# A threshold search in a two-layer kernel: counting on VectorE, or comparing on VectorE and adding up on TensorE

## The reference

```python
# layer 0, attention: 8 heads of 16
scores = einsum('bhqd,bhkd->bhqk', q, k) * scale * 1.25
threshold = top_k(scores, 102)[0][..., -1:]        # the 102nd largest of each row of 512
scores = scores * where(scores >= threshold, 1.24, 1.0)
li = conv1d(scores.mean(axis=-2), conv_w) + conv_b
probs = softmax(scores * li[:, :, None, :]);  x = x + ga * (probs @ v @ Wo + bo)
# layer 0, experts: all 8 experts on all tokens, mixed with top-2 weights
# layer 1: a Mamba block (a scan over 512 tokens, 256 channels, 16 states),
#          then 8 experts that each see at most 153 tokens of a batch (gather, three products, scatter)
```

## Time and profile before

| | us |
|---|---|
| median of three runs | 3173.97 (3163.5 to 3178.97) |
| the profiled execution, its own time | 3173.85 |
| its span in the trace | 3172.5 |
| VectorE busy | 2473.1 (78%) |
| TensorE busy | 2230.1 (70%) |
| ScalarE busy | 1472.9 (46%) |
| GpSimd busy | 1231.8 (39%) |

### The profile page before, as it was taken

The page is one execution under the profiler, slowest core; times in us unless marked ns, Lnnn a source line. Parts: engine busy times, 40 slices in busy tenths (PEclk is TensorE's granted clock), DMA queues, the critical chain, the costliest instruction groups (busy, mean ns, idle before and its releaser), DMA issues. The chain is left out here.

```text
span 3172.5 us, 33555 instructions
## 1 busy us (share of the span) xinstructions
PE 2230.1 (70%) x8648; PEld 1159.3 (37%) x8767; DVE 2473.1 (78%) x6145; ACT 1472.9 (46%) x3124; POOL 1231.8 (39%) x1118
## 2 busy tenths in 40 slices
PE   4168775877767777687768778677868778758644
PEld 2025221553235522454225532345325432435213
DVE  5874888869887799978889797889889897853472
ACT  3317613665245733567236732567236743724322
POOL 1020345414453054523545144532535144534461
PEclk7579786998878788897979889788969889869757
DMA  4011113141132212332121312323122321313223
GB/s 98 1 29 28 29 32 93 44 112 59 52 86 59 90 51 62 95 80 71 51 82 63 97 52 62 92 66 97 51 75 68 95 62 46 97 49 105 77 64 92
DMA packets 137460, 215.11 MB, mean 68 GB/s; under 512 B 17873, under 2 KB 57441, under 8 KB 134113
## 3 DMA queue, kind: packets, MB, share of 16 engines
q1 hardware_dynamic: 133088, 203.88, 22.6%
q0 software_dynamic: 4096, 8.40, 1.0%
HBM read 190.06 MB, written 22.15 MB: 67 GB/s over the span
## 5 line engine op out<-in xcount | busy, mean ns | idle before, releaser
L1370 POOL TENSOR_TENSOR gat<-sil,cbs 128x512 f32<-128x512 f32 x256 | 324.6, 1271 | 214.1 <-PE ps_rest L1300 109.6
L1335 ACT ACTIVATE sil<-ps_rest,w_b1T 128x512 f32<-128x512 f32 x256 | 175.5, 687 | 426.9 <-PE ps_rest L1310 405.0
L768 DVE TENSOR_SCALAR_CACHE_REDUCE wmask<-z,tc 128x512 bf16<-128x512 f16 x512 | 349.8, 740 | 30.3 <-ACT z L735 28.3
L1021 PE MATMUL ps_att<-z,Vp 128*32 128x128 f32 x2048 | 280.2, 283 | 46.0 <-DVE z L1093 33.5
L937 POOL TENSOR_SCALAR wmask<-wmask 128x512 bf16<-128x512 bf16 x256 | 164.3, 642 | 375.2 <-DVE wmask L894 369.3
L1310 PE MATMUL ps_rest<-rest_hT,WF 128*128 128x512 f32 x512 | 289.1, 652 | 16.1 <-ACT sil L1335 16.1
L1300 PE MATMUL ps_rest<-gat,WP 128*128 128x512 f32 x512 | 276.9, 625 | 12.2 <-POOL gat L1370 11.6
L1622 POOL TENSOR_TENSOR rest_c<-rest_c,hg 128x512 f32<-128x512 f32 x128 | 162.3, 1268 | 315.4 <-DVE hg L1581 315.4
L1549 ACT ACTIVATE ps_rest<-cols,Aneg 128x512 f32<-128x512 f32 x256 | 175.5, 688 | 225.4 <-DVE hfc L1569 197.6
L1021 PEld LDWEIGHTS ps_att<-z,Vp 128*32 128x32 f32 x2048 | 208.4, 112 | 135.3 <-issue 113.4
L1526 PE MATMUL ps_rest<-hg,ident 128*128 128x512 f32 x256 | 183.8, 808 | 102.9 <-DVE hg L1581 102.6
(11 more groups left out here) (347 smaller groups left out, 4976.5 us busy)
## 6 DMA issues: line engine op xcount, KB each, us to landing
cbs<-spreads SPq DMA_DIRECT2D x128, 256.0 KB, 3.6
ccs<-spreads SPq DMA_DIRECT2D x128, 256.0 KB, 3.3
WF<-in_w SPq DMA_DIRECT2D x64, 256.0 KB, 2.7
WP<-in_w SPq DMA_DIRECT2D x64, 256.0 KB, 2.7
WF<-in_wfc SPq DMA_DIRECT2D x64, 256.0 KB, 2.7
WG<-in_wgate SPq DMA_DIRECT2D x64, 256.0 KB, 3.0
WP<-in_wproj SPq DMA_DIRECT2D x64, 256.0 KB, 3.1
qk<-bounce SPq DMA_DIRECT2D x32, 384.0 KB, 5.8
```

The source lines that it names most:

```text
L768: od.up(dve.tensor_scalar(wmask[:, i, :], z_at[i], tc[:, 0, i:i + 1], None, ALU.is_ge, ALU.add, accum_out=tc[:, 1, i:i + 1]))
L1021: mm = pe.matmul(obank[o:o + 32, a * P:(a + 1) * P], Vp[:, kc, h, :], pT[u][:, kc, :], start=kc == 0, stop=kc == NT - 1)
L1370: weighed0.up(pool.tensor_tensor(gat[m % 2], sil[m % 2], cbs[e % 2][:], ALU.mult))
```

## The change

A tile is counted on VectorE no more in one instruction. VectorE writes the mask alone (`tensor_scalar` with `is_ge` and no `accum_out`). TensorE then takes the masks of a group of tiles, `FOLDS`, through an identity matrix: for a group of 16 tiles it multiplies, 16 times over, a slice of 32 columns of each mask, and accumulates all in one PSUM bank, so that 512 columns hold 32 partial sums for each tile. Groups of 8 or 6 tiles take slices of 64 columns, 8 times over. VectorE reduces each bank to counts with one `tensor_reduce`. Groups by round: 16 and 8 tiles, 16 and 6, 16 and 6, then 16, 8 and 8. ScalarE counts 8, 10, 10 and 0 tiles, in place of 8, 14, 14 and 0. The new generator `pe_search` stands in TensorE's list and waits there for the last compare of a group (`cut`), in round 0 also for the end of the refill before the second group; `dve_search` waits for the products (`spread`). `weave` is given 459.0 and a lead of 1.25 for the attention chain. Two more GpSimd instructions at the start make the identity in bf16.

```diff
-SIGNS = (8, 14, 14, 0)
+SIGNS = (8, 10, 10, 0)
 SLOPE = 1.0 / 140.0
 ROUNDS = len(SIGNS)
+FOLDS = {22: ((0, 16), (16, 22)), 24: ((0, 16), (16, 24)), 32: ((0, 16), (16, 24), (24, 32))}
+FOLD_W = {16: 32, 12: 32, 10: 32, 8: 64, 6: 64}
...
+    ident_bf = sb("ident_bf", [P, P], BF16)
...
+    cut, spread = sig("cut", sum(TILES - n for n in SIGNS)), sig("spread", sum(len(FOLDS[TILES - n]) for n in SIGNS))
...
+        built.up(pool.memset(ident_bf[:], 0.0)); pool.wait_ge(*built.at(0, 18))
+        built.up(pool.affine_select(out=ident_bf[:], in_=ident_bf[:], compare_op=ALU.not_equal, fill=1.0, base=0,
+                                    pattern=[[-1, P]], channel_multiplier=1))
...
+    def fold_bank(n):
+        return att.bank[3 - n]
+
+    def cut_before(k):
+        return sum(TILES - n for n in SIGNS[:k])
+
+    def spread_before(k):
+        return sum(len(FOLDS[TILES - n]) for n in SIGNS[:k])
+
+    def pe_search(b):
+
+        for k in range(ROUNDS):
+            for n, (lo, hi) in enumerate(FOLDS[TILES - SIGNS[k]]):
+                if k == 0 and n == 0 and b:
+                    yield attended.at(b - 1)
+                    pe.wait_ge(*attended.at(b - 1))
+                if k == 0 and n == 1:
+                    yield zed.all(b)
+                    pe.wait_ge(*zed.all(b))
+                yield cut.at(b, cut_before(k) + hi - 1)
+                pe.wait_ge(*cut.at(b, cut_before(k) + hi - 1))
+                w = FOLD_W[hi - lo]
+                to = fold_bank(n)[:, 0:(hi - lo) * w].rearrange("p (i w) -> p i w", w=w)
+                for c in range(S // w):
+                    mm = pe.matmul(to, ident_bf[:], wmask[:, lo:hi, c * w:(c + 1) * w], start=c == 0, stop=c == S // w - 1)
+                    if c == S // w - 1:
+                        spread.up(mm)
+                    yield 0.26
...
                     dve.wait_ge(*zed.at(b, i))
-                od.up(dve.tensor_scalar(wmask[:, i, :], z_at[i], tc[:, 0, i:i + 1], None, ALU.is_ge, ALU.add,
-                                        accum_out=tc[:, 1, i:i + 1]))
-                yield 0.67
+                cut.up(dve.tensor_scalar(wmask[:, i, :], z_at[i], tc[:, 0, i:i + 1], None, ALU.is_ge))
+                yield 0.27
+            for n, (lo, hi) in enumerate(FOLDS[TILES - SIGNS[k]]):
+                w = FOLD_W[hi - lo]
+                yield spread.at(b, spread_before(k) + n)
+                dve.wait_ge(*spread.at(b, spread_before(k) + n))
+                od.up(dve.tensor_reduce(tc[:, 1, lo:hi], fold_bank(n)[:, 0:(hi - lo) * w].rearrange("p (i w) -> p i w", w=w), AX.X, ALU.add))
+                yield 0.66
...
+    def pe_searches():
+        for b in every:
+            yield from pe_search(b)
...
-           (453.0, 1.1, (("pe", pe_choices()), ("act", act_choices()), ("dve", dve_choices()), ("pool", pool_choices()),
+           (459.0, 1.25, (("pe", pe_choices()), ("act", act_choices()), ("dve", dve_choices()), ("pool", pool_choices()),
                          ("pe", pe_attention()), ("act", act_attention()), ("dve", dve_attention()), ("pool", pool_attention()),
-                         ("sp", sp_attention()), ("pe", pe_prepares()), ("act", act_prepares()), ("dve", dve_prepares()), ("pe", pe_refills()), ("act", act_refills())))),
+                         ("sp", sp_attention()), ("pe", pe_prepares()), ("act", act_prepares()), ("dve", dve_prepares()), ("pe", pe_refills()), ("act", act_refills()), ("pe", pe_searches())))),
```

More of the change, by code:

```diff
@@ L136, in emit @@
     loaded, late = sig("loaded", len(EARLY) + 1, 16), sig("late", len(LATER), 16, 30.0)
-    built, hot, cleared = sig("built", 18), sig("hot", 8), sig("cleared", 8 * FULL + 2 * E + 7)
+    built, hot, cleared = sig("built", 20), sig("hot", 8), sig("cleared", 8 * FULL + 2 * E + 7)
     siluc, modp, bop, ready = sig("siluc", 2), sig("modp", 2), sig("bop"), sig("ready", 5)
```

## The result

The changed kernel takes **3417.14 us** (median of 4 runs, 3416.52 to 3429.65) against 3174.52: a ratio of 1.078 (95% interval 1.074 to 1.082), slower by 243 us. The forecast was 3095, with a range of 3010 to 3200 and a chance of 0.18 for slower.

The account below looks back on a forecast made before the run. VectorE was the fullest engine (2473 of 3172 us), though none was full over the whole span. Terms of -14 - 4 - 1.4 + 5 + 3 = -11.4 us a batch, -80 for seven, gave 3095 us, range 3010 to 3200.

Parts of the forecast that it names:

- Order and lead: Attention chain's lead of 1.25 for 1.1: attention at most 54 us earlier, costed at 0, with 20 us either way.
- The rest of the sum: All terms but the lead: -14 - 4 - 1.4 + 5 + 3 = -11.4 us a batch, -80 for seven.
- Counts, compares, reductions, ScalarE: Search: VectorE -61.4 + 27.0 + 5.9 = -28.5 us a batch; eight ScalarE counts fewer, -5.6, counted as -1.4.
- TensorE: 104 added products a batch in the search, taken at 0.275 us each, mostly in idle time: 3 us a batch show.
- Round latency: Search rounds 1 to 3 end behind the products yet get shorter: -14 us a batch, between -8.3 and -20.3.
- The second rival: No change: rounds wait for products in TensorE's list, so the gains sum to zero, 3174 us; chance 0.17.
- Collision with GpSimd: Beside exp0, GpSimd keeps 250 compares waiting 0.25 us each, 62 us in all; counted as +5 us a batch.
- The third rival: Slower: GpSimd keeps VectorE's compares out in rounds 2 and 3 beside exp0, 3254 or 3304 us; chance 0.18.

Follow-up runs that it names:

- constant lead: Changed kernel with attention's planned work per batch set to 435.6 in place of 459.0, so 1.25 does not grow over the batches: 3093.24 us, ratio 0.976.
- the Identity pair: Changed kernel with exp0's Silu replaced by Identity: 3319.38 us with 459.0 and 1.25, 3096.59 us with 435.6 and 1.25.
- the cut of TensorE's work: Changed kernel, exp0's second product for 128 of 512 columns: 3233.48 us at 459.0, 1.25 with Identity for Silu; 3067.97 us at 453.0, 1.1 with Silu.
- the same repair: Kernel before with attention's planned work 443.1 and 1.25 in place of 453.0 and 1.1: 3088.72 us, ratio 0.976.
- the old settings: Changed kernel with 453.0 and a lead of 1.1, as in the kernel before, in place of 459.0 and 1.25: 3143.81 us, ratio 0.992.
- the run at 3247: Changed kernel with compares that still sum, into an unused tile, with 475.6 planned and a lead of 1.25 that does not grow: 3247.40 us, ratio 1.024.

## Why the prediction was wrong

**The step that failed** is "Order and lead", costed at 0 with 20 us either way. It cost 273 us: 3417 against 3144, the changed kernel with the new settings and with the old ones. Against a constant lead it is 324. I took the lead for a shift of at most 54 us, a question of how long the end is. I did not add up the planned work, so I missed that 459.0 makes the lead grow, to 1.66 at the last batch where the kernel before has 1.28, and I did not ask which stages would meet. The end that I had named but priced at nothing went from 376 to 484 us. Two more of the things that follow could be read ahead of time: that Silu and Exp alternate on one engine, from the lines of ScalarE's list, and that the scan needs VectorE for 69 of 73 us and exp0 TensorE for 60 of 62, so that each must lie beside something that leaves this engine free.

Of the 324 us the loads are 98, shown by the Identity pair. The 223 of the distance are shown as a sum, and that 112 of them lie in the end is read from the traces. That the others come from stages that want the same engine side by side is what the stretches suggest; the cut of TensorE's work didn't prove it, and what does most there stays open.

**The rest of the sum** came out at 3093 against the 3095 of the forecast (its terms add up to 3094), and that is luck: the kernel before comes to 3089 by the same repair, and at the old settings the change was worth 30 us (3144), not 80. So the other terms failed in size too. The two pages at the constant lead, kernel before and changed kernel:

```profile
PE 2200.5 (71%) x8767; PEld 1136.5 (37%) x8767; DVE 2449.8 (79%) x6145; ACT 1473.9 (48%) x3124; POOL 1229.5 (40%) x1118
```

```profile
PE 2365.4 (76%) x9599; PEld 1210.5 (39%) x9599; DVE 2258.7 (73%) x5545; ACT 1431.5 (46%) x2996; POOL 1235.8 (40%) x1120
```

VectorE has 191 us less to do and the span is 11 us longer (3082.7 and 3094.0; the medians differ by 4).

- *Counts, compares, reductions, ScalarE:* right in size. 0.27 a compare, 0.684 a reduction, VectorE's busy sum down by 183 where 165 was forecast.
- *TensorE:* a product takes 0.22 as said, and the busy sum rose by 152 to 165, less than the 180 to 350 forecast. By themselves the products cost 25 us; I had 3 us a batch, 21 in seven. In the first batch's rounds the granted clock is 0.75, where it was 0.50 with TensorE idle:

```profile
83.00:136.00 53.00, 24.59 (x87) 9.69 (x88) 35.13 (x133) 15.99 (x46) 0.47 (x1) 0.75 0.00 1
```

- *Round latency:* wrong. I had rounds 1 to 3 shorter by 14 us, 9 with the collision. At a constant lead the three rounds of batch 4 go from 1372.80 to 1456.89 in the kernel before and from 1362.49 to 1443.46 in the changed one, 84.1 and 81.0 us. Batches 2 to 7 are alike, about 3 us a batch less in the mean. Round 1 even grew, from 26.9 to 37.7. In the changed kernel itself batch 3 took 18.6, 21.4 and 27.7 us, where 16 to 18 twice and 18 were forecast, but ahead of exp0, which starts at 1130.7 there, and not beside it. The timeline of VectorE in the changed kernel, constant lead, from the end of round 0 to that of round 1:

```profile
1362.49 0.17 DVE L816 TENSOR_SCALAR tc<-tc 128x8 f32<-128x8 f32 x1
...
1378.93 0.34 DVE L804 TENSOR_SCALAR wmask<-both_parts,tc 128x512 bf16<-128x512 f16 x1
...
1397.87 0.69 DVE L810 TENSOR_REDUCE tc<-ps_att 128x16 f32<-128x512 f32 x1 [0.89 <-PE ps_att L785]
...
1400.22 0.16 DVE L816 TENSOR_SCALAR tc<-tc 128x10 f32<-128x10 f32 x1
```

and TensorE's in the same kernel:

```profile
1373.35 0.59 PE L785 MATMUL ps_att<-wmask,ident_bf 128*128 128x512 bf16 x2
...
1374.94 0.38 PE L785 MATMUL ps_att<-wmask,ident_bf 128*128 128x512 bf16 x1
1375.19 0.53 PE L1793 MATMUL ps_rest<-cols,WF 128*128 128x153 f32 x2
...
1392.36 0.38 PE L785 MATMUL ps_att<-wmask,ident_bf 128*128 128x512 bf16 x1
...
1393.52 1.89 PE L785 MATMUL ps_att<-wmask,ident_bf 128*128 128x512 bf16 x8
...
1397.46 0.86 PE L785 MATMUL ps_att<-wmask,ident_bf 128*128 128x512 bf16 x4
...
1362.00:1400.00 38.00, 33.87 (x196) 28.17 (x197) 27.18 (x94) 23.93 (x61) 2.05 (x2) 0.88 0.40 123
```

  The last compare ends at 1379.3; the reduction starts 18.6 us later. The 24 products want 5 us, but they stand in pieces among the products of exp1 (L1793): three run by 1375.3, the next only at 1392.36, with 17 us of exp1 between, on a TensorE that is busy for 34 of 38 us (last row, busy by stretch). I had priced the products back to back, at 0.275 each. The second rival had this mechanism, rounds that wait for TensorE; its price, no change, is what the constant lead shows.
- *Collision with GpSimd:* right in kind, and the size, 70 us of VectorE's time against 62, fits by luck. I had 250 compares beside exp0 at 0.25 more each. In the changed kernel none lies in exp0. There 71 take over 0.6 us, about 1 us more each, all beside GpSimd's products of the scan (L1650, L1663):

```profile
1775.30 1.26 POOL L1663 TENSOR_TENSOR rest_c<-rest_c,hg 128x512 f32<-128x512 f32 x1 [7.93 <-DVE hg L1622]
1776.50 2.72 DVE L804 TENSOR_SCALAR wmask<-z,tc 128x512 bf16<-128x512 f16 x2
1776.52 1.27 POOL L1650 TENSOR_TENSOR rest_c<-cols,cbs 128x512 f32<-128x512 f32 x1
1777.74 1.32 POOL L1650 TENSOR_TENSOR gat<-cols,cbs 128x512 f32<-128x512 f32 x1
```

  At the constant lead rounds do lie beside exp0, and the excess is 21 us over all compares (mean 372 ns), a third of the forecast, with 9 compares over 0.6 us. The third rival, slower by this collision, is refuted as the main cause: the kernel before, whose counts were never hit, loses 147 us by the same settings. But the 49 us between 70 and 21 are VectorE time in a scan where VectorE is nearly full, so a part of the 223 us may be theirs. No run separates it.

## What to carry to other kernels

When independent chains share the engines, decide which stages may lie side by side before anything is tuned: by the engine each fills, and by the function table ScalarE needs in each. A number that sets the order (a lead, a total of planned work) must be made anew with every change of a planned duration, and a change has to be compared with the kernel before at the best order found for each; else it is the order that is measured, up to 324 us here against 30 at the old settings and 4 at the constant lead for the change. Work that is moved to another engine's queue costs the wait behind what stands there, not its own duration.

## What the runs showed of the hardware

- Two ScalarE functions from two tables cost 1.283 us at each change, and next to nothing beside it: in the timeline above a load starts 0.02 us behind the accumulator's read (2404.07 + 0.19 to 2404.28), and the activation follows 1.29 us after it. The Trainium skill (ScalarE: Activation LUTs, § What ACT_TABLE_LOAD costs) gives the same 1283 ns and a drain of about 1380 more; that drain is not seen here, and the measurement decides. In time the 180 loads were worth 98 us.
- An instruction of the fast form waits for GpSimd where the summing form of the same comparison never did: up to 1.445 us against a median of 0.345, and 0.748 at most for the sum. With the products and reductions of the change beside it (the run at 3247) the summing form stays at 0.747 at most as well. The longest compare, 3.114 us at the constant lead, lies over two GpSimd instructions in a row. By line, then with two more compares behind it and GpSimd beside them:

```profile
L804 DVE TENSOR_SCALAR wmask<-both_parts,tc x192: 329/346/3114, 68.5 to 2502.1; 128x512 bf16<-128x512 f16 x192
...
1783.51 3.64 DVE L804 TENSOR_SCALAR wmask<-both_parts,tc 128x512 bf16<-128x512 f16 x3
1783.95 2.51 POOL L1411 TENSOR_TENSOR gat<-sil,cbs 128x512 f32<-128x512 f32 x2
```

- TensorE takes a moving operand in pieces of 32 columns, 1024 bytes apart, at the rate of a contiguous one, 0.22 us for 512 columns at a granted clock of 1.00 (1397 to 1401 us of the changed kernel).
